# Macaron block (routed FFN, selective scan, routed FFN): a reordering of the scan stage over TensorE, VectorE, GpSimd and ScalarE

## The reference

```python
x = x + 0.5 * ffn(layernorm(x))     # 8 experts, top 1, and one shared expert
x = x + scan(layernorm(x))          # 16 states per channel
x = x + 0.5 * ffn(layernorm(x))
```

```python
x_proj = x @ W_x.T                                  # 64 + 16 + 16 columns
dt_x, Bm, Cm = split(x_proj)
dt = softplus(dt_x @ W_dt.T + b_dt)
dA = exp(einsum('bld,dn->bldn', dt, -exp(A_log)))
dBx = einsum('bld,bln,bld->bldn', dt, Bm, x)
h_t = dA_t * h_{t-1} + dBx_t                        # along the 512 tokens
y_t = sum_n h_t * C_t ;  y = y + x * D
```

## Time and profile before

| | us |
|---|---|
| median of 3 runs | 442.29 (442.14 to 442.9) |
| the profiled execution, its own time | 441.44 |
| its span in the trace | 439.6 |
| scan stage in the trace, 64 steps | 186.6 (142.8 to 329.4) |
| busy in the span: PE, DVE, POOL, ACT | 402.4, 329.5, 281.1, 275.0 |
| granted TensorE clock, mean | 0.996 |

### The profile page before, as it was taken

How to read it: one execution, slowest core, us unless ns; L and a number is a source line. 1 busy time by engine, 2 the same in 40 slices (tenths; PEclk the granted TensorE clock), 3 DMA queues, 4 the chain that set the end, 5 groups by cost and what they waited for, 6 DMA issues and landing times. The chain is left out here.

```text
span 439.6 us, 8329 instructions
## 1 busy us (share of the span) xinstructions
PE 402.4 (92%) x2716; PEld 278.4 (63%) x2716; DVE 329.5 (75%) x518; ACT 275.0 (63%) x501; POOL 281.1 (64%) x216
## 2 busy tenths in 40 slices
PE   6899899999996899899989997989999899899995
PEld 5537444444454689777977797879994556344452
DVE  4678565553388988999999999989887775456552
ACT  1430465564248799897999899997962210556553
POOL 7204356643328589997999799988891006487553
PEclk9899999999999999999999999999999999999999
DMA  8958115842604226463536453443320534334311
GB/s 250 385 179 264 48 54 167 284 174 101 204 10 91 73 82 180 81 144 106 186 75 118 141 176 73 115 157 92 121 72 0 172 107 120 99 118 135 111 60 48
DMA packets 50808, 56.84 MB, mean 129 GB/s; under 512 B 16329, under 2 KB 35597, under 8 KB 50768
## 3 DMA queue, kind: packets, MB, share of 16 engines
q1 hardware_dynamic: 46624, 45.78, 35.0%
q0 software_dynamic: 4144, 10.54, 8.0%
HBM read 41.14 MB, written 16.48 MB: 131 GB/s over the span
## 5 line engine op out<-in xcount | busy, mean ns | idle before, releaser
L523 POOL TENSOR_TENSOR gs<-hs,c_sb 128x1024 f32<-128x1024 f32 x63 | 148.3, 2380 | 18.7 <-DVE hs L1421 11.4
L1421 DVE TENSOR_TENSOR_SCAN hs<-da,bank 128x1024 f32<-128x1024 f32 x64 | 144.1, 2273 | 4.1 <-PE bank L1030 2.1
L663 ACT ACTIVATE da<-dt_sb,a_neg 128x511 f32<-128x511 f32 x128 | 84.5, 713 | 2.4 <-DVE dt_sb L1384 1.2
L1054 PE MATMUL bank<-ident,gs 128*128 128x128 f32 x504 | 66.3, 275 | 7.5 <-POOL gs L523 5.9
L1054 PEld LDWEIGHTS bank<-ident,gs 128*128 128x128 f32 x504 | 55.9, 141 | 12.1 <-POOL gs L523 9.8
L679 ACT ACTIVATE dbx_t<-dtx_t,h_sb 128x256 f32<-128x256 f32 x145 | 62.1, 498 | 1.6 <-DVE dtx_t L1390 1.4
L879 PE MATMUL bank<-xnT,w_gu 128*128 128x512 f32 x112 | 50.8, 601 | 0.0
L1030 PE MATMUL bank<-ident,dbx_t 128*128 128x128 f32 x336 | 44.2, 274 | 6.8 <-DVE hs L1421 4.1
L477 POOL DMA_INDIRECT da<-rows,row_token x29 | 30.6, 1055 | 29.7 <-DVE row_token L1292 21.2
L1030 PEld LDWEIGHTS bank<-ident,dbx_t 128*128 128x128 f32 x336 | 37.5, 141 | 12.2 <-DVE hs L1421 5.9
L591 ACT ACTIVATE th<-bank,da 128x256 f32<-128x256 f32 x36 | 17.0, 473 | 43.1 <-PE bank L918 30.4
(11 more groups left out here) (184 smaller groups left out, 787.1 us busy)
## 6 DMA issues: line engine op xcount, KB each, us to landing
c_sb<-c_dram SPq DMA_DIRECT2D x64, 256.0 KB, 3.3
rows<-xn_no SPq DMA_DIRECT2D x8, 516.0 KB, 5.4
diag_dram<-dbx_t SPq DMA_DIRECT2D x6, 512.0 KB
routing<-diag_dram SPq DMA_DIRECT2D x11, 256.0 KB, 2.8
slot_m<-diag_dram SPq DMA_DIRECT2D x11, 256.0 KB, 2.9
rows<-xn_no SPq DMA_DIRECT2D x1, 2064.0 KB, 9.4
x_sb<-in_x SPq DMA_DIRECT2D x4, 512.0 KB, 6.4
w_gu<-in_gate_w SPq DMA_DIRECT2D x2, 1024.0 KB, 10.2
```

The lines of the kernel that those rows point to most:

```text
L523: nc.gpsimd.tensor_tensor(gs[:, s % 2], hs[:, s % RING], c_sb[:, s % RING].unsqueeze(1).to_broadcast([P, KC, L]), ALU.mult).then_inc(sc_g, 1)
L663: nc.scalar.activation(da[:, s % RING, k, 1:L], dt_sb[:, k, seq(s // N)][:, 1:L], ACT.Exp, scale=a_neg[:, k, s % N:s % N + 1]).then_inc(sc ...
L1054: mm = nc.tensor.matmul(YA[k][:, i * P:(i + 1) * P], products[:, k, i * P:(i + 1) * P], ident[:], start=(s % N == 0 and i == 0), stop=(s % ...
L1421: nc.vector.tensor_tensor_scan(hs[:, s % RING].rearrange(flat), da[:, s % RING].rearrange(flat), DBX[s % 2][:, :, :].rearrange(flat), 0.0, ...
```

## The change

Five edits, all about the scan stage.

1. At n = 0 of batches 1 to 3 TensorE issues `add(s - 1)` ahead of `turn_dbx(s + 2)` and not behind it.
2. ScalarE loads the table set "natural_log_exp_and_others" in place of that for Exp, and loads it once more behind the Tanh of `shared_gate(0, 3, 1)`, ahead of the first `decay`.
3. `DIAG` names other states of batches 0, 1 and 2, six each as before, not side by side.
4. `BY_DVE` gives VectorE no tiles from n = 6 on: two tiles fewer in batch 0, three fewer in batches 1 and 2.
5. Batches 0 and 1 are normalised for the second FFN by ScalarE at n = 6 to 9 of the following batch, in place of GpSimd at n = 5 to 8; `shift` runs in each batch from 1 on. The second of the four pieces moves from n = 3 to n = 2 in batch 3.

```diff
-    BY_DVE = ((2, 2, 2, 1, 1, 1) + (0,) * 6 + (1, 0, 1, 0),) + ((1, 1, 0, 1) + (0,) * 6 + (1, 0, 1, 0, 1, 0),) * 2 + ((0,) * 16,)
-    DIAG = (tuple(range(6, 12)),) + (tuple(range(4, 10)),) * 2 + ((4, 7, 9, 13),)
+    BY_DVE = ((2, 2, 2, 1, 1, 1) + (0,) * 10,) + ((1, 1, 0, 1) + (0,) * 12,) * 2 + ((0,) * 16,)
+    DIAG = ((6, 7, 9, 10, 12, 14),) + ((4, 6, 7, 9, 11, 13),) * 2 + ((4, 7, 9, 13),)
...
-    PIECES = (0, 3, 6, 12)
+    PIECES = (0, 2, 6, 12)
+    EXP_LN = "natural_log_exp_and_others"
...
             def shift(b):
                 pool.wait_ge(ln_rstd, BATCH * 2 + b + 1)
+                if b > 0:
+                    pool.wait_ge(ln_xn, 2 * GT + LT * b)
...
-                    if b == BATCH - 1 and n == 3:
+                    if b > 0 and n == 3:
                         shift(b - 1)
-                    if 0 < b < BATCH - 1 and 5 <= n < 5 + LT:
-                        normalise(2, b - 1, (n - 5,))
...
             def normalise(b, i):
                 if i == 0:
-                    act.wait_ge(ln_shift, 1)
+                    act.wait_ge(ln_shift, b + 1)
...
-                    if not more and 6 <= n < 6 + LT:
+                    if b > 0 and 6 <= n < 6 + LT:
                         normalise(b - 1, n - 6)
...
-            nc.scalar.preload_act_table(ACT.Exp)
+            nc.scalar.preload_act_table_set(EXP_LN)
...
             shared_gate(0, 3, 1)
+            nc.scalar.preload_act_table_set(EXP_LN)
             act.wait_ge(a_ready, 2)
...
+                    if b > 0 and n == 0:
+                        add(s - 1)
                     if s + 2 < STATES:
                         turn_dbx(s + 2)
...
-                    if s > 0:
+                    if n > 0:
                         add(s - 1)
```

## The result

The changed kernel takes 437.91 us (median of 6 runs, 437.15 to 439.87) against 441.9 us for the kernel before (6 runs). The ratio is 0.9924, 95% interval 0.9905 to 0.9943: faster by 0.76%, some 3.4 us. The profiled execution took 437.5 us, its span is 435.8 against 439.6.

What follows compares the result with a forecast made beforehand. VectorE's own list was taken as the bound in batches 1 and 2, with TensorE nearer in batch 3. Terms summed to 4.45, say 4.6 us, giving 436.8 for the profiled execution and a median of 437.7, range 435.2 to 441.0 us.

Steps and rivals of the forecast that it cites:

- VectorE is the bound of batches 1 and 2: In batches 1 and 2 VectorE, 97% and 98% busy, was taken to set the pace with its own list.
- Tiles, 8 x 0.31 = 2.5: Eight tiles of 0.31 us leave VectorE's list in batches 0 to 2, a gain of 2.5 us.
- Turns, 2.5: At the three inner batch turns, add issued first removes VectorE's waits ahead of add_y, a gain of 2.5 us.
- The cap in batch 0: GpSimd's unbroken products let at most 1.15 us of batch 0's gain through, a term of -0.4 us.
- The Ln wait in batch 1: ScalarE's Ln in batch 1 ends late, so VectorE waits 0.65 us instead of 0.3; 0.35 off the gain.
- The table load in batch 3: One 1.29 us load before the first tanh_piece makes VectorE's hidden_piece wait 0.6 us (0 to 1.3).
- The spread, 0.2: Alternating diagonal with plain states in batches 0 to 2 relieves TensorE's diagonal turns, gaining 0.2 us.
- Batch 3, 0.2: The second piece at n = 2 fills TensorE's gap in batch 3, gaining 0.2 us.
- ScalarE's work: ScalarE's busy time forecast at 44.3 us in batch 1 and 43.1 in batch 2, level with VectorE.
- ScalarE paces batches 1 and 2 in part: Rival: half of ScalarE's waits for TensorE stay on top of its work, losing 2.4 us, 440.1 us; chance 0.20.
- ScalarE's lead is used up: Rival: all of ScalarE's waits for TensorE stay, kernel slower by 2.5 us, 444.8 us; chance 0.07.
- Better than the sum: Rival: waits for ScalarE vanish, batch 0's cap gives way, new set holds Tanh: gain 6.9, 435.4 us; chance 0.12.

Runs made afterwards that it cites:

- u_tiles: Changed kernel with VectorE making the eight tiles of later states again: stretch 1.56 us longer, 440.79 us, ratio 0.9952 to the kernel before.
- b_tiles: Kernel before with one edit, no VectorE tiles from n = 6 on: stretch 0.16 us shorter, 442.30 us, ratio 0.9990 to the kernel before.
- u_turn: Changed kernel with add behind turn_dbx again at n = 0 of batches 1 to 3: stretch 1.24 us longer, 440.36 us, ratio 0.9947 to before.
- i_tanh_ln: Changed kernel with batch 3's first tanh_piece and batch 1's Ln issued earlier on ScalarE: stretch 180.24 against 181.10 us, 437.29 us, ratio 0.9921 to before.
- u_diag_tiles: Changed kernel with diagonal states side by side and eight tiles on VectorE again: stretch 2.25 us longer, 441.49 us, ratio 0.9979 to before.
- u_tables: Changed kernel with the Exp table set loaded as before, two loads around each Ln: stretch 4.53 us longer, 443.69 us, ratio 1.0019 to before.
- u_diag: Changed kernel with diagonal states side by side again in batches 0 to 2: stretch 4.35 us longer, 442.37 us, ratio 1.0029 to before.
- b_spread: Kernel before with diagonal states spread, two batch 0 tiles moved to plain states: stretch 3.30 us longer, 444.65 us, ratio 1.0062 to before.
- i_tanh: Changed kernel with batch 3's first tanh_piece issued ahead of state 52's decay on ScalarE: stretch 0.10 us longer, 437.84 us, ratio 0.9913 to before.
- i_preload: Changed kernel with earlier first Tanh, earlier batch 1 Ln and the Tanh table load issued by itself: stretch 179.24 us, 436.87 us, ratio 0.9871 to before.

## Why the prediction was right, and where its steps were not

The forecast was 437.7 us and the measurement 437.91. The agreement is closer than the steps deserve: the gain was forecast at 4.6 us and is 3.2 us in the stretch, 3.4 by the ratio. Two accidents hid the difference. The median of before moved from 442.29 to 441.9 with more runs; and the medians lie 4.0 us apart, more than the scans explain. In the profiled executions the spans differ by 3.8 us, of which 0.6 is that the first scan started earlier, and that start varies by 2.6 us from run to run.

- **VectorE is the bound of batches 1 and 2**: right for the changed kernel, 44.12 of 45.48 and 43.25 of 43.35 us.
- **Tiles, 8 x 0.31 = 2.5**: the price is right (1.0 us for three tiles, u_tiles), the six in batches 1 and 2 count, the two in batch 0 are hidden, as the cap had it. But it is 1.56 only beside the other edits, and 0.16 alone (b_tiles).
- **Turns, 2.5**: the three waits are gone; the edit is worth 1.24, for half of what it frees is then waited for ScalarE.
- **The cap in batch 0**: forecast 1.15 us of gain at scan 18; measured (198.78 - 142.78) - (197.12 - 142.15) = 1.03. It is a cap indeed: scan 18 starts 54.94 to 54.98 us after the first in all nine kernels that have the new order at the turns and the new table set, whatever their tiles and diagonal states in batch 0; with the old order at the turn it starts at 55.83 (u_turn, b_tiles), one plain turn later. One way in which it acts shows in two lines (TensorE, VectorE): TensorE waits for GpSimd's product, the diagonal turn behind it comes late, and VectorE waits.

```profile
183.02 1.09 PE L1056 MATMUL bank<-ident,gs 128*128 128x128 f32 x8 [1.56 <-POOL gs L526]
...
186.38 2.29 DVE L1425 TENSOR_TENSOR_SCAN hs<-da,bank 128x1024 f32<-128x1024 f32 x1 [0.57 <-PE bank L1039]
```

What I missed is that the cap reaches on. GpSimd's late products hold TensorE's adds, these hold `project(2)`, and ScalarE waits for that, 0.91 us at 192.86 (first line; then VectorE in batch 1):

```profile
192.86 0.59 ACT L631 ACTIVATE th<-bank 96x512 f32<-96x512 f32 x1 [0.91 <-PE bank L985]
...
208.13 0.70 DVE L1374 SCALAR_TENSOR_TENSOR bank<-bank,w_exp 128x512 f32<-128x512 f32 x1 [0.36 <-ACT bank L651]
...
211.83 0.70 DVE L1385 TENSOR_TENSOR bank<-tt,bank 128x512 f32<-128x512 f32 x1 [0.82 <-ACT tt L658]
```

- **The Ln wait in batch 1**, forecast 0.65, measured 0.82, and 0.36 more for the copy: 0.5 us of the 1.4 that are missing. The chain from the cap to this wait is argued from the trace, not tried; that the Ln stands behind the decay and tiles of state 24 was tried, and moving it ahead of them took its wait away (i_tanh_ln).
- **The table load in batch 3**: a load stands before the first Tanh, as I had taken it, at 1.30 us start to start (287.23 to 288.53); VectorE's wait for it was put at 0.6 and is 1.08, another 0.5 us. The rest of the 1.4 is in small gaps that no run here separates. The load at the start cost nothing, as forecast: ScalarE waits 1.23 us behind it.

```profile
132.56 1.28 ACT L577 ACT_TABLE_LOAD   x1
...
134.47 1.28 ACT L759 ACT_TABLE_LOAD   x1
136.98 1.33 ACT L664 ACTIVATE da<-dt_sb,a_neg 128x511 f32<-128x511 f32 x2 [1.23 <-DVE dt_sb L1388]
```

- **The spread, 0.2**: the step that failed. I priced it on TensorE, by the waits for diagonal turns, and on ScalarE I looked only at the tiles that it puts ahead of Ln. It is mainly ScalarE's edit: a diagonal state is one for which ScalarE makes no tiles, and without the spread ScalarE falls behind by the end of batch 2 once it has VectorE's tiles as well (u_diag_tiles). What GpSimd's normalising, which ScalarE also took over, adds to that was not tried. The spread is worth 4.35 in the changed kernel, and -3.30 alone in the kernel before, where it pushes tiles and a load ahead of Ln.
- **Batch 3, 0.2**: the piece is worth 0.06, and the batch kept its 45.60 us: the turn's wait that left was replaced by that for the Tanh.
- **ScalarE's work**, put at 44.3 and 43.1 us in batches 1 and 2, is 43.52 and 42.54: level with VectorE, as forecast, and a little under it. Of the other signs, no load stands around Ln, and GpSimd's 40.19 and 38.51 us are near the 39 forecast.
- **The rivals.** "ScalarE paces batches 1 and 2 in part" names much of what ate the gain, and the 3.2 to 3.4 us measured are no nearer to the forecast's 4.6 than to its 2.2. Its mirror, that ScalarE's lead is used up, did not happen in the changed kernel, and did as soon as one of the edits that relieve it was taken out (u_tables, u_diag). "Better than the sum" fell on all its conditions: the cap held, the waits for ScalarE stayed, and the Tanh needed its load.

The edits' worths when undone add up to 1.24 + 4.53 + 2.39 + 1.56 + 4.35 + 0.06 = 14.1 us against a total of 3.2. They are not terms of a sum: two take work off VectorE and GpSimd and put it on ScalarE, and two (tables, spread) make the room for it. The spread alone doesn't pay (b_spread), and the tiles alone meet the sum at the turns first (b_tiles); the other edits were not tried alone.

## What to carry to other kernels

When four engines are all near 90% busy or above, don't price an edit by the waits that it removes today; write for each engine what the edit gives it and when, and look at the engine that receives work: an edit that seems to be worth 0.2 us may be what lets the others pay. Judge a bundle as a bundle: two of its parts were tried alone here, and one was even and one slower. And issue a table load by itself ahead of a wait, so that it runs while the engine would be idle.

## What the runs showed of the hardware that was not expected

The table load that comes with the first activation of a new set is executed behind that activation's semaphore wait: 1.05 us idle, then 1.28 us of load (i_tanh); issued by its own call ahead of the wait, the same load of 1.28 us left VectorE without a wait (i_preload, 1.00 us less). And the part ahead of the scans, with the same work up to about 132 us, varied by 2.6 us from one profiled execution to another, while batch 0 of the scans repeated to within 0.04 us in seven of them.
